# Edge loop of a graph network in steps of two slices and two subtiles, with 1024 columns in one instruction

## What is computed

```python
def mish(x):
    return x * jnp.tanh(jax.nn.softplus(x))
edge_feat = jnp.concatenate([x[src], x[dst], edge_attr], axis=-1)
h = mish(edge_feat @ W1 + b1)
messages = mish(h @ W2 + b2)
agg = jax.ops.segment_sum(messages, dst, num_segments=x.shape[0])
u = mish(jnp.concatenate([x, agg], axis=-1) @ W3 + b3)
out = u @ W4 + b4
```

## Time and profile before

| | before |
|---|---|
| median of 3 runs | 1516.39 us (1514.3 to 1517.26) |
| span of the profiled execution | 1514.7 us |
| TensorE busy | 1490.6 us, 98% |
| VectorE busy | 1413.2 us, 93% |
| ScalarE busy | 1303.0 us, 86% |
| GpSimd busy | 1077.3 us, 71% |
| mean granted clock of TensorE | 0.997 of full speed |

### The profile page before, as it was taken

How to read it: one execution, slowest core, us unless ns; L and a number is a source line. 1 busy time by engine, 2 the same in 40 slices (tenths; PEclk the granted TensorE clock), 3 DMA queues, 4 the chain that set the end, 5 groups by cost and what they waited for, 6 DMA issues and landing times.

```text
span 1514.7 us, 33348 instructions
## 1 busy us (share of the span) xinstructions
PE 1490.6 (98%) x7862; PEld 1166.5 (77%) x7862; DVE 1413.2 (93%) x2920; ACT 1303.0 (86%) x2510; POOL 1077.3 (71%) x978
## 2 busy tenths in 40 slices
PE   7989999999999999999999999999999999999998
PEld 6766777777777777777777777777777777777885
DVE  7889999999999999999999999999999999996676
ACT  5088999999999999999999999999999999996562
POOL 1266888788788888878888887888878788863320
PEclk9999999999999999999999999999999999999999
DMA  8866555455555555555555555554555555554773
GB/s 292 271 218 171 120 124 119 114 127 123 119 118 125 118 117 127 122 119 118 125 118 117 124 124 120 118 125 118 116 125 124 120 118 125 118 128 100 175 167 148
DMA packets 124757, 205.10 MB, mean 135 GB/s; under 512 B 31642, under 2 KB 57370, under 8 KB 124721
## 3 DMA queue, kind: packets, MB, share of 16 engines
q0 software_dynamic: 58528, 112.91, 35.1%
q1 hardware_dynamic: 65840, 91.24, 19.5%
q10 hardware_dynamic: 352, 0.52, 0.1%
HBM read 151.60 MB, written 42.75 MB: 128 GB/s over the span
## 4 chain that ended last, share of the span: by engine, by line
PE 94%; DVE 3%; ACT 1%; DMA 1%; issue 1%; SPq 0%; POOL 0%; POOLq 0%; DVEq 0%; ACTq 0%
PE bm L1158 56%; PE bp L1137 7%; PE bp L1145 6%; PE bs L1181 5%; PE bp L1147 5%; PE pm L1169 2%; PE pu L336 2%; PE po L2146 2%; PE pu L2124 2%; PE pB L723 2%; PE pA L723 2%; PE pm L1168 2%; PE pu L2191 1%; DMA M_tab<-zero 1%; PE pu L2178 1%
## 5 line engine op out<-in xcount | busy, mean ns | idle before, releaser
L1062 POOL TENSOR_TENSOR hTl<-tp,hTh 128x512 fp32r<-128x512 f32 (+1 forms) x314 | 414.3, 1319 | 153.6 <-DVE khl L1357 152.8
L1158 PE MATMUL bm<-W2h,hTh 128*128 128x512 f32 x1252 | 499.4, 399 | 1.1 <-DVE bm L1350 0.5
L1158 PE MATMUL bm<-W2l,hTh 128*128 128x512 f32 x1252 | 497.1, 397 | 0.0
L1158 PE MATMUL bm<-W2h,hTl 128*128 128x512 f32 x1252 | 494.6, 395 | 0.0
L1049 POOL DMA_INDIRECT xg<-A_tab,idx x305 | 324.0, 1062 | 102.8 <-issue 79.7
L1158 PEld LDWEIGHTS bm<-W2h,hTh 128*128 128x128 f32 x1252 | 235.7, 188 | 73.3 <-DVE bm L1350 18.7
L1158 PEld LDWEIGHTS bm<-W2l,hTh 128*128 128x128 f32 x1252 | 235.5, 188 | 57.3
L1158 PEld LDWEIGHTS bm<-W2h,hTl 128*128 128x128 f32 x1252 | 235.6, 188 | 53.6
L1217 ACT ACTIVATE rp<-bp 128x512 f32<-128x512 f32 (+1 forms) x314 | 183.8, 586 | 100.4 <-PE bp L1147 98.9
L1321 DVE SCALAR_TENSOR_TENSOR rp<-rp 128x512 f32<-128x512 f32 (+1 forms) x314 | 214.8, 684 | 29.5 <-issue 13.4
L1331 DVE SCALAR_TENSOR_TENSOR tp<-rp,bp 128x512 f32<-128x512 f32 (+1 forms) x314 | 211.8, 675 | 7.6 <-POOL hTl L1062 2.8
(11 more groups left out here) (248 smaller groups left out, 2308.9 us busy)
## 6 DMA issues: line engine op xcount, KB each, us to landing
ea<-in_eaT SPq DMA_DIRECT2D x156, 128.0 KB
M_tab<-mev POOLq DMA_DIRECT2D x157, 80.0 KB, 6.3
agg_tab<-ev POOLq DMA_DIRECT2D x157, 64.0 KB, 2.5
db<-in_dst_rows SPq DMA_DIRECT2D x78, 128.0 KB
M<-M SPq DMA_DIRECT2D x76, 128.0 KB
M_tab<-zero SPq DMA_DIRECT2D x10, 640.0 KB
xg<-A_tab,idx POOLq DMA_INDIRECT x313
eaW<-Bh_tab SPq DMA_DIRECT2D x77, 64.0 KB
```

Of the source, the lines that this page charges most:

```text
L1062: e.tensor_tensor(hTl[p][:, j, 0:w], pick(u, start_t, tp)[:, 0:w], hTh[p][:, j, 0:w], ALU.subtract)\
L1158: last = e.matmul(bank[0:r, :], a[p][:, c, j * P:j * P + r], w[:, c, :], start=False, stop=c == KC - 1 and w is W2l, skip_group_check=True)
```

## The change

The slots are taken in pairs. In a step s (even) TensorE transposes and multiplies slices s+4 and s+5, then subtiles s and s+1, then adds both to M. The pairs of buffers `rp`, `rm` and `tp` become one tensor of two halves each, the two banks `bp` one of two banks, the four banks `bm` one of four. ScalarE's Ln and Exp of the slices, and Square, Ln and Exp of the subtiles, and VectorE's square, products and rounding take both halves, 1024 columns, in one instruction. Both Exp that read PSUM (L1217 and L1237 before) and the writing of the bias stay at 512 columns. Each stage has its own semaphore. The loop runs from step 18 on. GpSimd no longer waits for `khl` ahead of a low part but for the rounding, and it does its two low parts behind its DMAs.

The core of the diff:

```diff
-def slots(eng, first, head, tail, last, step):
-
-    for s in range(first, head):
+def pairs(eng, first, head, tail, last, step):
+
+
+    for s in range(first, head, 2):
         step(At(None, s))
     with eng.Fori(head // (2 * SUB), tail // (2 * SUB)) as i:
-        for k in range(2 * SUB):
+        for k in range(head % (2 * SUB), head % (2 * SUB) + 2 * SUB, 2):
             step(At(i, k))
-    for s in range(tail, last):
+    for s in range(tail, last, 2):
...
-    PRE_AHEAD = 5
-    ACT_MSG = 1
-    DVE_PRE = 4
-    DVE_MSG = 2
-    SEG_LAG = 3
-    PREP_AHEAD = (9, 8, 6)
-    GATHER_AHEAD = {1: (11, (0,)), 2: (10, (1,)), 3: (9, (2,)), 0: (8, (3,))}
-    EV_LAG = 7
-    ACC_LAG = 8
-    ONE_LAG = 2
+    AHEAD = 4
+    BEHIND = 2
+    PREP_AHEAD = (10, 8, 6)
+    SEG_LAG = 6
+    EV_LAG = 8
+    ACC_LAG = 10
     ACCS = 2
     MBUF = 2 * SUB
-    ADJ_AHEAD = 1
     ADJ_EV_LAG = 4
-    ADJ_LAG = {2: (6, 0), 0: (8, 1)}
-    BACK = 2
-    FIRST, LOOP0 = -10, 16
-    LOOP1 = 4 * FULL - 16
-    LAST = 4 * NG + EV_LAG + 2
+    ADJ_LAG = 6
+    LOOP0 = 18
+    LOOP1 = 4 * FULL - 14
+    LAST = 4 * NG + ACC_LAG
...
-        rp = [sb(f"rp{i}", [P, G]) for i in range(2)]
-        rm = [sb(f"rm{i}", [P, H]) for i in range(2)]
-        tp = [sb(f"tp{i}", [P, G]) for i in range(2)]
-        tm = [sb(f"tm{i}", [P, H]) for i in range(MBUF)]
+        rp = sb("rp", [P, 2, G])
+        rm = sb("rm", [P, 2, H])
+        tp = sb("tp", [P, 2, G])
+        tm = sb("tm", [P, MBUF, H])
...
+        bp = ps("bp", (P, 2 * G))
         pm = ps("pm")
-        bm = [ps(f"bm{i}") for i in range(4)]
+        bm = ps("bm", (P, SUB * H))
...
+        def banks_free(u):
+
+            return 4 if u.reg is None and u.const == SUB else u.val(2, -2)
...
+                u, q = s + AHEAD, s + -SEG_LAG
+                if u.has(PRES):
+                    e.wait_ge(v_pre, banks_free(u))
+                    for n in range(2):
+                        gathered(u + n, bank(u + n))
+                    for n in range(2):
+                        products(u + n, bank(u + n))
+                for n in range(2):
+                    if (s + n).has(MSGS):
+                        msg(s + n)
+                for n in range(2):
+                    if (s + n).has(MSGS):
+                        adjacency(s + n)
...
+            def pre_exp(u):
...
+                e.wait_ge(v_pre, banks_free(u))
+                for n in range(2):
+                    e.wait_ge(s_pre, u.val(1, n + 1))
+                    e.activation(rp[:, n, 0:w], bank(u + n)[:, 0:w], ACT.Exp, bias=LNSQ).then_inc(a_exp, 1)
+
+            def pre_rest(u):
+
+                t = rp[:, :, 0:ETAIL if tail(u) else G]
+                e.wait_ge(v_sq, u.val(1, 2))
+                e.activation(t, t, ACT.Ln, bias=1.0, scale=0.5 / (SQ * SQ)).then_inc(a_ln, 2)
+                e.wait_ge(a_ln, u.val(1, 2))
+                e.activation(t, t, ACT.Exp, scale=-1.0).then_inc(a_rho, 2)
...
+            def msg_exp(m):
+
+                r, n = ETAIL if tail(m) else P, m.const % 2
+                wait(e, v_msg, m.val(1, -n))
+                e.wait_ge(s_msg, m.val(1, 1))
+                e.activation(rm[0:r, n, :], message(m.j, r), ACT.Exp).then_inc(a_mexp, 1)
+
+            def pair_of(m):
+
+                return rm[0:ETAIL, 0:1, :] if tail(m) else rm[:, :, :], 1 if tail(m) else 2
+
+            def msg_square(m):
+
+                t, n = pair_of(m)
+                e.wait_ge(a_mexp, m.val(1, n))
+                e.activation(t, t, ACT.Square, bias=SQ, scale=SQ).then_inc(a_msq, n)
+
+            def msg_ln(m):
+
+                t, n = pair_of(m)
+                e.wait_ge(a_msq, m.val(1, n))
+                e.activation(t, t, ACT.Ln, bias=0.5, scale=0.5 / (SQ * SQ)).then_inc(a_mln, n)
+
+            def msg_rho(m):
+
+                t, n = pair_of(m)
+                e.wait_ge(a_mln, m.val(1, n))
+                e.activation(t, t, ACT.Exp, scale=-1.0).then_inc(a_mrho, n)
...
+                u, m, q, g = s + AHEAD, s + -BEHIND, s + -EV_LAG, s + -ADJ_EV_LAG
+                if (m + 1).has(MSGS):
+                    msg_exp(m + 1)
+                if g.j == 0 and g.has(MSGS):
+                    adjacency(g)
+                if m.has(MSGS):
+                    msg_square(m)
+                if u.has(PRES):
+                    pre_exp(u)
+                if m.has(MSGS):
+                    msg_ln(m)
+                if u.has(PRES):
+                    pre_rest(u)
+                if m.has(MSGS):
+                    msg_rho(m)
+                if s.has(MSGS):
+                    msg_exp(s)
+                if s.reg is None and s.const == 4 * FULL + 2:
+                    evac(At(None, 4 * FULL - SUB))
+                elif q.j == 0 and q.has(4 * FULL - SUB):
+                    evac(q)
...
+            def pre(u):
+
                 w = ETAIL if tail(u) else G
-                t = pick(u, start_r, rp)[:, 0:w]
-                e.wait_ge(a_pre, exps(u, 0))
-                e.scalar_tensor_tensor(t, t, 2.0 * SQ, t, ALU.add, ALU.mult).then_inc(v_sq, 1)
-
-            def pre(u, k):
+                e.wait_ge(a_rho, u.val(1, 2))
+                e.wait_ge(g_pre, 2 if u.reg is None and u.const == SUB else u.val())
+                e.scalar_tensor_tensor(tp[:, :, 0:w], rp[:, :, 0:w], 1.0, both(bp, w), ALU.subtract, ALU.mult)\
+                 .then_inc(v_pre, 2)
...
+                r, n = (ETAIL, 1) if tail(m) else (P, 2)
+                o = m.const % MBUF
                 wait(e, s_seg, m.group(1, -1))
-                e.wait_ge(a_msg, m.val(4, 4))
-                e.scalar_tensor_tensor(tm[m.const % MBUF][0:r, :], rm[m.const % 2][0:r, :], 1.0, bm[m.j][0:r, :],
-                                       ALU.subtract, ALU.mult).then_inc(v_msg, 1)
+                e.wait_ge(a_mrho, m.val(1, n))
+                e.scalar_tensor_tensor(tm[0:r, o:o + n, :], rm[0:r, 0:n, :], 1.0,
+                                       message(m.j, r, n).rearrange("p (k n) -> p k n", k=n),
+                                       ALU.subtract, ALU.mult).then_inc(v_msg, n)
 
             def bias(m):
 
-                e.wait_ge(v_msg, m.val(1, 1))
-                e.tensor_copy(bm[m.j][:, :], b2b[:]).then_inc(v_bias, 1)
+                e.wait_ge(v_msg, m.val(1, 2 - m.const % 2))
+                e.tensor_copy(message(m.j, P), b2b[:]).then_inc(v_bias, 1)
...
+                u, m, q, h = s + AHEAD, s + -BEHIND, s + -EV_LAG, s + -SUB
                 if u.has(PRES):
-                    pre(u, 0)
-                if v.has(PRES):
-                    square(v)
-                if u.has(PRES):
-                    pre(u, 1)
+                    square(u)
+                if not (s.reg is None and s.const == 0):
+                    for n in range(2):
+                        if (s + n).has(MSGS):
+                            adjacency(s + n)
                 if s.reg is None and s.const == 0:
                     prep(At(None, 2 * SUB), 0)
                 for k in range(3):
                     g = s + PREP_AHEAD[k]
                     if g.j == 0 and g.has(4 * NG):
                         prep(g, k)
-                if (s + ADJ_AHEAD).has(MSGS) and not (s.reg is None and s.const == 0):
-                    adjacency(s + ADJ_AHEAD)
-                if f.has(MSGS - SUB):
-                    bias(f)
+                if h.j == 0 and h.has(MSGS) and not (h.reg is None and h.const <= SUB):
+                    onehot(h)
+                if u.has(PRES):
+                    pre(u)
+                    high(u)
                 if m.has(MSGS):
                     msg(m)
-                h = s + -ONE_LAG
-                if h.j == 0 and h.has(MSGS) and not (h.reg is None and h.const <= SUB):
-                    onehot(h)
-                q = s + -(EV_LAG + 2)
-                if q.j == 0 and q.has(MSGS):
-                    if tail(q):
-                        e.wait_ge(s_seg, NG)
-                        e.sem_inc(s_fin, 1)
+                for n in range(2):
+                    if (m + n).has(MSGS - SUB):
+                        bias(m + n)
```

264 lines of the change are left out of this document (119 added, 145 removed).

## The result

The changed kernel takes 1852.26 us (median of 4 runs, 1852.01 to 1853.54); the kernel before, run beside it, 1516.58 (1514.30 to 1517.26). The ratio is 1.2216, 95% interval 1.2202 to 1.2231. It was predicted as 1784 us with a range of 1745 to 1860. The profiled execution has a span of 1851.9 us at a mean granted clock of 0.995.

What follows compares the result with a forecast made beforehand. A turn of waits between ScalarE and VectorE, 10.07 us a pair against 8.29, was taken to bind; 98.4 + 1530.6 + 15.4 + 9.4 ends the last message product at 1653.8, the span at 1782.4, plus 1.7: 1784 us, range 1745 to 1860.

Steps and rivals of the forecast that it cites:

- the hand-overs: Delay from an instruction's end to the start of the one needing it, on ScalarE and VectorE: 0.04 us each.
- The loop of waits: ScalarE and VectorE, from one message product's end to the next: every pair costs a whole turn, 10.07 us on average.
- Wide instructions: 1024 columns, interpolated from narrower and wider records: 1.05 us on ScalarE, 1.22 for VectorE's two-input operation.
- I take 0.04: Chosen delay in us before a dependent instruction starts, from 0.03 to 0.04 seen, up to 0.10 from ScalarE to VectorE.
- The bound of 0.10: Hand-overs at 0.10 us instead of 0.04, four of them 0.24 a turn, in the case of a longer turn.
- They are just hidden: VectorE's one-hot tiles and preparation, 2.19 us, fit beside ScalarE's Ln and Exp, where 2.30 are free.
- The whole: Sum over the run: first message product ends at 98.4 us, 152 turns take 1530.6, last product ends at 1653.8.
- The stages behind it don't change: Work after the last message product, which ended at 1386.10 us in the kernel before, keeps its time.
- The longer turn: Rival: wide instructions dear as two narrow, 0.55 us a turn (1868 us), or slower hand-overs, 0.24; chance 15%.
- The clock: Rival: TensorE's clock falls and stays at 1.2 GHz, about 2756 us; chance 4%. The forecast expected it near 1.00.
- The turn did bind: Against the rival that the turn, at most 8.2 us, doesn't bind and TensorE decides: 1498 us; chance 5%.
- VectorE's share: Sign expected in the profile: VectorE busy near 80% of the span.

Runs made afterwards that it cites:

- 1: Changed kernel with the messages' chain worked in place in `tm`, so `rm` is out of it: 1610.88 us, ratio 1.0628.
- 4: Changed kernel with each wide instruction as two of 512 columns, each waiting for its own half alone: 1643.56 us, ratio 1.0843.
- 5: Changed kernel with order swapped: message product ahead of pre product on VectorE, same swap on ScalarE, buffers kept: 1629.79 us, ratio 1.0746.
- 2: Changed kernel with `rp` given four halves and the pre product in place in it, `tp` gone, `rm` kept: 1853.14 us, ratio 1.2226.
- version 3: Changed kernel with each wide instruction as two of 512 columns, both still waiting for the whole pair: 1881.95 us, ratio 1.2416.
- the mixed version: Changed kernel with the slices' whole chain narrow, half by half, and the messages' chain wide and in place in `tm`: 1585.77 us, ratio 1.0458.
- 12: Changed kernel with messages in place in `tm`, slices narrow by halves, GpSimd's low parts behind its second adding DMA, ahead of its second gather: 1517.03 us, ratio 1.0007.

## Why the prediction was right, point by point

- *The forecast.* 1852 us is 68 above the 1784 forecast and 8 below the top of the range. The mechanism held, and some 56 of the 68 us come from one term of the turn, the hand-overs, as the points below show.
- *The loop of waits* was right in every link, in the order given. 120 turns from the message product at 402.40 to that at 1659.54 are 10.48 us each, against 10.07 predicted and 8.29 before. That its link through `rm` binds was tested from two sides: with the link cut (1), or half by half (4), or shortened by the order (5), 209 to 241 us come back; with the other buffer doubled (2), none.
- *Wide instructions* at 1.05 and 1.22: measured 1.06 and 1.21 to 1.23. Here are three groups of the changed kernel, 400 to 1600 us:

```profile
L1386 DVE SCALAR_TENSOR_TENSOR tp<-rp,bp 128x1024 f32<-128x1024 f32 x115 | 140.4, 1221 | 30.4 <-issue 28.9
...
L1395 DVE CAST hTh<-tp 128x1024 fp32r<-128x1024 f32 x115 | 79.9, 694 | 11.1
...
L1243 ACT ACTIVATE rp<-rp 128x1024 f32<-128x1024 f32 x115 | 122.0, 1060 | 10.5
```

- *"I take 0.04"* is the term that was mis-sized. From 400 to 1000 us of the changed kernel (57 turns, timelines) five links end in a wide waiter in every turn. They take 0.09 (Ln and Exp), 0.10 (square and rounding) and 0.12 (pre product) on average. A sixth, into the Square, takes 0.09 in every second turn; in the others the copy `mev` covers it. The narrow Exp behind the message product takes 0.04 and 0.11 in turn. What is over 0.04 in these adds up to 0.37 of the 0.41 us by which a turn is longer than in the sum; the rest is instructions that are a hundredth or two longer each. The bound of 0.10 stood in the prediction, but with four links (0.24).
- *"They are just hidden"*, of VectorE's one-hot tiles and preparation, is nearly so, but 2.19 us was too low: in the turn shown they take 2.53 (806.68 to 809.21) and end 0.14 after ScalarE's Exp (809.07), and the pre product starts at 809.27, 0.20 after the Exp. This is so in 14 of 58 turns, in the others 0.10. It is in the 0.12 above.
- *The whole.* The first message product ends at 100.29 (99.08 + 1.21), 1.9 later than taken. The last ends at 1716.70, so the loop took 1616.4 us against 1555.4 in the sum, 61 more, what the turn explains: 152 x 0.41 = 62. *"The stages behind it don't change"* was wrong by 6.6 us (135.2 against 128.6). TensorE waits once, 6.01 us, for VectorE's `aTl`. In VectorE's order that stands behind a copy of the last sum into `ev`, which waits 10.90 us for an adding DMA to land; in the kernel before that wait is 3.87 us and TensorE doesn't wait. Why the DMA lands later, counted from the last message product, wasn't tested. 1782.4 + 1.9 + 61.0 + 6.6 is the span of 1851.9. The first and the last message product of the changed kernel, and then the copy:

```profile
99.08 1.21 DVE L1403 SCALAR_TENSOR_TENSOR tm<-rm,bm 128x1024 f32<-128x1024 f32 x1
```

```profile
1716.02 0.68 DVE L1403 SCALAR_TENSOR_TENSOR tm<-rm,bm 64x512 f32<-64x512 f32 x1 [1.22 <-ACT rm L1272]
```

```profile
1728.43 0.68 DVE L1429 COPY ev<-bs 32x512 f32<-32x512 f32 x1 [10.90 <-DMA agg_tab<-ev]
```

The same copy in the kernel before:

```profile
1392.12 0.68 DVE L1369 COPY ev<-bs 32x512 f32<-32x512 f32 x1 [3.87 <-DMA agg_tab<-ev]
```

TensorE in the changed kernel:

```profile
1729.83 1.97 PE L2173 MATMUL pt<-ident,ag 128*128 128x128 f32 x8 [6.01 <-DVE aTl L2022]
```

- *The rivals.* The longer turn came close in size (1868 against 1852), but by its second reason, the hand-overs. Its first, wide instructions as dear as two narrow ones, is refuted by the 1.06 and 1.22. So the forecast's mechanism held, with one of its terms at the rival's value. The clock stayed at 1.00, its higher level, from 100 to 1600 us, with waits of TensorE's matmuls of 1.4 us at most; where it did fall in the loop, in version 3, no turn got longer. The turn did bind. Of the signs named, VectorE's share is off: 76% and not 80%.
- *What was not foreseen.* Once the loop is cut, the kernel isn't back at 1516 but at 1611 or 1630. In the mixed version the rest is VectorE held up by GpSimd's low parts, as 12 shows; in the swapped one the square's 0.55 us a pair points to the same, without such a test. In the kernel before, the low parts wait for the one-hot tiles (99.2 us of waits in the earlier trace rows) and so run beside the bias, the message product and the pre product. The prediction saw the change drop that wait and read it only as an earlier start. In the changed kernel the square still keeps its 1.22 us, because the low parts run beside other work and idle time of VectorE.
- *Open.* Which of version 12's three edits are needed was not told apart: the wide version in place (1) with GpSimd's order of 12 wasn't run. In version 1 the square's mean is 1435 ns, 0.2 us of waiting a pair, and its pair takes 0.6 us more than the 8.29 before; the other 0.4 isn't settled. Nor is it settled whether the 0.10 comes from the 1024 columns or from their pattern of two pieces.

## What to carry to other kernels

Before two instructions are merged into one, follow the buffer: a double buffer used whole is a single one, and each merged unit then pays the whole round trip through all engines that touch it. Price that round trip from the trace and compare it with the bound engine's time for the same unit; the fixed cost spared is small beside it. Work moved out of one loop can land in another, and beside another engine's work that stops it, so a move has to be priced at its new place too.
